# A quantised feed-forward at the end of a four-layer network: its tokens taken by blocks and eighths, its rounding on ScalarE

## The reference, cut to what matters

```python
def _affine_quantize(x):
    amin, amax = (jnp.min(x), jnp.max(x))
    scale = jnp.maximum((amax - amin) / 255.0, 1e-08)
    zp = jnp.clip(jnp.round(-amin / scale) + QMIN, QMIN, QMAX)
    q = jnp.clip(jnp.round(x / scale) + zp, QMIN, QMAX)
    return (q, scale, zp)

def _qlinear(x, W, b):
    xq, sx, zx = _affine_quantize(x)
    wq, sw = _sym_quantize(W)
    acc = jnp.einsum('bsh,oh->bso', xq - zx, wq)
    return acc * (sx * sw) + b
h = _qlinear(x, W1, b1)          # 256 -> 1024 features
h = jax.nn.gelu(h, approximate=False)
out = _qlinear(h, W2, b2)        # 1024 -> 256 features
...
x = x + _L3_ffn_ref(_L3_cond_ref(x, ...), W1, b1, W2, b2)
```

## Time and profile before

| | us |
|---|---|
| three runs | 2984.24, 2985.74, 2986.35 |
| the profiled execution | 2986.55 |
| its span, first to last instruction | 2985.2 |
| from the last extreme of y3 (2895.9) to the end of the span | 89.3 |
| of these, VectorE busy | 72.2 |

### The profile page before, as it was taken

One profiled execution on the slowest core, in us unless ns is written; L12 is line 12 of the kernel. 1 busy time (PEld: TensorE's weight loads), 2 busy tenths in 40 slices (PEclk: granted clock), 3 DMA queues, 4 the chain that ended last, 5 costly groups with the idle time before them and its releaser, 6 DMA issues.

```text
span 2985.2 us, 150990 instructions
## 1 busy us (share of the span) xinstructions
PE 2734.0 (92%) x59732; PEld 2284.0 (77%) x59732; DVE 2077.2 (70%) x12188; ACT 1613.8 (54%) x8443; POOL 338.9 (11%) x457
## 2 busy tenths in 40 slices
PE   7689999999999999999999999998679999979984
PEld 4478999989989899998999989878556666744331
DVE  6688888877777777777777777665456666665238
ACT  3445555566666666666666666543335555511115
POOL 0000101101001010010100101001024444410000
PEclk7555555555555555555555555555589999979997
DMA  3142323212123221231212312101568665251000
GB/s 132 39 118 84 98 73 93 88 38 82 59 75 97 61 83 58 76 92 59 85 55 76 95 57 89 32 14 45 211 222 259 196 193 170 74 175 53 1 0 28
DMA packets 170143, 270.95 MB, mean 91 GB/s; under 512 B 23353, under 2 KB 125644, under 8 KB 167140
## 3 DMA queue, kind: packets, MB, share of 16 engines
q1 hardware_dynamic: 125524, 202.29, 21.6%
q0 software_dynamic: 15312, 33.67, 3.3%
q10 hardware_dynamic: 28608, 25.35, 3.1%
HBM read 170.77 MB, written 98.70 MB: 90 GB/s over the span
## 4 chain that ended last, share of the span: by engine, by line
PE 84%; DVE 8%; ACT 4%; issue 2%; DMA 1%; SPq 0%; POOL 0%; POOLq 0%; ACTq 0%; DVEq 0%
PE work L678 9%; PE bank_h L688 7%; PE bank_r L688 7%; PE bank_z L688 7%; PE bank_g L688 7%; PE bank_h L697 5%; PE work L688 5%; PE bank_r L697 4%; PE bank_z L697 3%; PE bank_g L697 3%; PE work L914 3%; PE bank_z L914 3%; PE bank_h L939 2%; PE work L939 2%; PE work L1025 2%
## 5 line engine op out<-in xcount | busy, mean ns | idle before, releaser
L688 PEld LDWEIGHTS work<-h_run,hi_r 128*128 128x128 f16 x4092 | 258.3, 119 | 164.8 <-DVE h_run L1783 150.0
L688 PE MATMUL work<-h_run,hi_r 128*128 128x2 f16 x4092 | 286.8, 174 | 65.3 <-DVE h_run L1783 60.9
L1783 DVE TENSOR_TENSOR_SCAN h_run<-z_run,hh_run 128x12 f16<-128x12 f32 x1024 | 186.8, 182 | 229.3 <-ACT hh_run L1224 210.5
L1224 ACT ACTIVATE hh_run<-bank_h 128x4 f32<-128x4 f32 x1024 | 179.2, 175 | 275.7 <-PE bank_h L697 275.0
L1205 ACT ACTIVATE r_guess<-work 128x4 f32<-128x4 f32 x1023 | 177.0, 173 | 236.0 <-PE work L688 218.7
L1768 DVE TENSOR_TENSOR_SCAN rh_run<-r_run,h_run 128x12 f16<-128x12 f32 x1023 | 187.1, 183 | 151.5 <-ACT r_run L1214 107.9
L688 PE MATMUL bank_g<-h_hi,hi_g 128*128 128x2 f16 x4092 | 253.4, 166 | 38.7 <-ACT h_hi L1194 38.1
L697 PE MATMUL bank_h<-rh_run,hi_h 128*128 128x2 f16 x4092 | 263.8, 169 | 1.8 <-DVE rh_run L1768 1.2
L1219 ACT ACTIVATE z_run<-bank_z 128x4 f32<-128x4 f32 x1024 | 180.3, 176 | 149.1 <-PE bank_z L697 4.2
L688 PE MATMUL bank_h<-h_run,hi_h 128*128 128x2 f16 x4092 | 253.7, 166 | 3.3 <-DVE h_run L1765 3.3
L697 PE MATMUL bank_g<-h_lo,hi_g 128*128 128x2 f16 x4092 | 253.2, 166 | 1.4 <-DVE h_lo L1746 0.5
(11 more groups left out here) (481 smaller groups left out, 8076.8 us busy)
## 6 DMA issues: line engine op xcount, KB each, us to landing
stage<-in_gate_up SPq DMA_DIRECT2D x128, 384.0 KB
stage<-in_down SPq DMA_DIRECT2D x128, 192.0 KB, 3.0
gu_split<-parts SPq DMA_DIRECT2D x64, 384.0 KB, 2.8
gu_ring<-gu_split SPq DMA_DIRECT2D x64, 384.0 KB
xt<-x_rows ACTq DMA_DIRECT2D x191, 128.5 KB, 2.2
x_rows<-zero_rows SPq DMA_DIRECT2D x64, 257.0 KB, 3.3
yk<-y_rows SPq DMA_DIRECT2D x16, 1024.0 KB, 4.8
dn_split<-parts SPq DMA_DIRECT2D x64, 192.0 KB, 2.7
```

The costliest lines, as they stand in the source:

```text
L688: ins = pe.matmul(o[:, m, step, :], w[:, k, m * P:(m + 1) * P], hi(k), start=False, stop=False, skip_group_check=True)
L1224: act.activation(two(t.hh_run[:, :, 1]), gate_in(t.h, c2, s2), ACT.Tanh, scale=scale_of["h"]).then_inc(s.hh_act, 1)
L1783: dve.tensor_tensor_scan(t.h2_run[:, 0:3 * KH * B], threes(t.z_run), threes(t.hh_run), 0.0, ALU.mult, ALU.add).then_inc(s.h2hi, 1)
```

## The change

- Step 2: ScalarE rounds `y3` block by block (2 x 512 elements a partition) as soon as the inverse is there (a semaphore `inv` on L2017); VectorE clips each block in two passes, and the first of them already writes bfloat16 into `xq`, the second works on `xq` in place. Blocks 2 and 3 are rounded and clipped in the midst of step 3: after the first piece, or pair of pieces, of the block before.
- Step 3: the block is outside and the feature piece inside. VectorE takes an extreme over two feature pieces (2 x 512 elements) in one instruction: 32 reductions.
- Steps 4 and 5: ScalarE rounds `h3` in eighths of the tokens (8 x 256 elements), as soon as the inverse is there; VectorE clips an eighth in two passes, the second in bfloat16. TensorE fills for each eighth the two halves of one bank with 16 matmuls of 256 columns; four banks are used in turn. VectorE multiplies the bank by `f2` and adds `xf` in one instruction for both halves, two eighths behind the clipping. ScalarE no longer evicts; b2 is added to `xf` by ScalarE ahead of step 2 (two instructions of 2048 elements a partition), behind the last Gelu of the layer's experts (L1289).
- The stores go by eighths, 8 of 256 KB as before.

```diff
@@ sync
+    for u in range(8):
+        sp.wait_ge(s.xo, u + 1)
+        sp.dma_start(halves(out)[:, :, eighth(u)], t.xf[:, :, eighth(u)]).then_inc(s.stores, 16)
@@ tensor
     for v in range(NI * NBLK):
-        m, j = divmod(v, NBLK)
+        j, m = divmod(v, NI)
+        if m == 0:
+            pe.wait_ge(s.xq, j + 1)
...
+    for u in range(8):
+        pe.wait_ge(s.hq, u + 1)
+        if u >= 4:
+            pe.wait_ge(s.xo, u - 3)
+        for m in range(KH):
+            for k in range(NI):
+                ins = pe.matmul(work[u % 4][:, m * EIGHTH:(m + 1) * EIGHTH], t.wq3["W2"][:, k, m * P:(m + 1) * P],
+                                t.hq[:, k, eighth(u)], start=(k == 0), stop=(k == NI - 1))
         ins.then_inc(s.o3_mm, 1)
@@ scalar
+    for m in range(KH):
+        act.activation(t.xf[:, m], t.xf[:, m], ACT.Identity, bias=t.b2c[:, m:m + 1])
+    def rounded_input(j):
+        y = t.y3[:, :, blk_cols(j)]
+        act.activation(y, y, ACT.Identity, bias=t.round_col, scale=t.affine["x"]["inv"]).then_inc(s.rounded, 1)
+    act.wait_ge(s.inv, 1)
+    rounded_input(0)
+    rounded_input(1)
     act.wait_ge(s.f1, 1)
     for v in range(NI * NBLK):
-        m, j = divmod(v, NBLK)
+        j, m = divmod(v, NI)
+        if m == 0 and 1 <= j < NBLK - 1:
+            rounded_input(j + 1)
...
-    act.wait_ge(s.f2, 1)
-    for j in range(NBLK):
-        h3 = t.h3[:, :, blk_cols(j)]
-        act.activation(h3, h3, ACT.Identity, bias=t.round_col, scale=t.affine["h"]["inv"]).then_inc(s.hround, 1)
-    for v in range(NBLK * KH):
...
-        act.activation(t.o3[v % 2], t.work[v % 2], ACT.Identity, bias=t.b2c[:, m:m + 1], scale=t.f2).then_inc(s.o3, 1)
+    act.wait_ge(s.inv, 2)
+    for u in range(8):
+        h3 = t.h3[:, :, eighth(u)]
+        act.activation(h3, h3, ACT.Identity, bias=t.round_col, scale=t.affine["h"]["inv"]).then_inc(s.rounded, 1)
@@ vector
+    def to_range(src, dst, tag, quantised):
+        a = t.affine[tag]
+        v.on(dve.tensor_scalar(dst, src, ROUND, a["lo"], ALU.subtract, ALU.max))
+        dve.wait_ge(v.sem, v.n)
+        dve.tensor_scalar(dst, dst, a["hi"], None, ALU.min).then_inc(quantised, 1)
...
+    quantised_input(0)
+    dve.tensor_tensor(t.f1, t.affine["x"]["scale"], t.w3_scale[:, 0:1], ALU.mult).then_inc(s.f1, 1)
+    quantised_input(1)
+    for i in range(NI // 2 * NBLK):
+        j, pair = divmod(i, NI // 2)
+        h3 = t.h3[:, 2 * pair:2 * pair + 2, blk_cols(j)]
+        dve.wait_ge(s.h3, 2 * i + 2)
+        dve.tensor_reduce(t.part[:, 0, i:i + 1], h3, AXXY, ALU.max)
+        v.on(dve.tensor_reduce(t.part[:, 1, i:i + 1], h3, AXXY, ALU.min, negate=True))
+        if pair == 0 and 1 <= j < NBLK - 1:
+            quantised_input(j + 1)
...
+    for u in range(8 + 2):
+        if u < 8:
+            dve.wait_ge(s.rounded, NBLK + u + 1)
+            to_range(t.h3[:, :, eighth(u)], t.hq[:, :, eighth(u)], "h", s.hq)
+        if u >= 2:
+            xc = t.xf[:, :, eighth(u - 2)]
+            dve.wait_ge(s.o3_mm, u - 1)
+            dve.scalar_tensor_tensor(xc, t.work[(u - 2) % 4].rearrange("p (m n) -> p m n", m=KH), t.f2, xc, ALU.mult,
+                                     ALU.add).then_inc(s.xo, 1)
```

More of the change, by code:

```diff
@@ L14 @@
 ACT = mybir.ActivationFunctionType
-AXX = mybir.AxisListType.X
+AXX, AXXY = mybir.AxisListType.X, mybir.AxisListType.XY
 RED = bass.bass_isa.ReduceOp
@@ L44 @@
 E3, H3, S3 = 8, 128, 512
+EIGHTH = N // 8
 NS3 = S3 // P
@@ L66 @@
 blk_cols = lambda j: slice(j * BLK, (j + 1) * BLK)
+eighth = lambda u: slice(u * EIGHTH, (u + 1) * EIGHTH)
 class Steps:
@@ L118 @@
     tb_mm tb router_mm scores comb_sb comb_mm combT sh_mm sg s_in
-    he_mm he_act he o2_mm y3 ext ar xq f1 h3_mm h3 f2 hround hq o3_mm o3 xo stores
+    he_mm he_act he o2_mm y3 ext ar inv rounded xq f1 h3_mm h3 hq o3_mm xo stores
     dve
@@ L429, in place_tiles @@
         t.h3 = sb("h3", [P, NI, N])
-        t.part = sb("part", [P, 2, NI * NBLK])
+        t.part = sb("part", [P, 2, NI // 2 * NBLK])
         t.round_col = sb("round_col", [P, 1])
         t.hq = sb("hq", [P, NI, N], BF16)
-        t.o3 = [sb(f"o3_{i}", [P, BLK]) for i in range(2)]
     dram = lambda name, shape, dt: nc.dram_tensor(name, shape, dt, kind="Internal").ap()
@@ L578, in sync_program @@
         sp.dma_start(t.yk[c % 3].rearrange("p k d -> p (k d)"), results_of[c]).then_inc(yk_sem(s, c), 16)
-    for v in range(NBLK * KH):
[L581 to L584, removed]
+    for u in range(8):
+        sp.wait_ge(s.xo, u + 1)
+        sp.dma_start(halves(out)[:, :, eighth(u)], t.xf[:, :, eighth(u)]).then_inc(s.stores, 16)
+    sp.wait_ge(s.stores, 16 * 8)
 def tensor_program(pe, A, t, s):
@@ L1035, in tensor_layer3 @@
                 ins.then_inc(s.o2_mm, 1)
-    pe.wait_ge(s.xq, 1)
     pe.wait_ge(s.wq3, 1)
     for v in range(NI * NBLK):
-        m, j = divmod(v, NBLK)
+        j, m = divmod(v, NI)
+        if m == 0:
+            pe.wait_ge(s.xq, j + 1)
         if v >= 6:
@@ L2016, in affine @@
         dve.wait_ge(v.sem, v.n)
-        v.on(dve.reciprocal(a["inv"], a["scale"]))
-        dve.wait_ge(v.sem, v.n)
+        dve.reciprocal(a["inv"], a["scale"]).then_inc(s.inv, 1)
+        dve.wait_ge(s.inv, at)
         v.on(dve.tensor_tensor(a["zp"], a["ar"][:, 1:2], a["inv"], ALU.mult))
@@ L2029, in affine @@
         dve.wait_ge(v.sem, v.n)
-    fl, ax = flat(t.y3), t.affine["x"]
+    def to_range(src, dst, tag, quantised):
[3 more added lines that the diff above has]
+        dve.tensor_scalar(dst, dst, a["hi"], None, ALU.min).then_inc(quantised, 1)
+    dve.memset(t.round_col, ROUND)
     dve.wait_ge(v.sem, last)
@@ L2034, in vector_layer3, with quantised_input @@
     affine("x", 1)
[L2035 to L2045, removed]
+    def quantised_input(j):
+        dve.wait_ge(s.rounded, j + 1)
+        to_range(t.y3[:, :, blk_cols(j)], t.xq[:, :, blk_cols(j)], "x", s.xq)
+    quantised_input(0)
[9 more added lines that the diff above has]
+            quantised_input(j + 1)
     dve.wait_ge(v.sem, v.n)
@@ L2048, in vector_layer3 @@
     affine("h", 2)
[L2049 to L2062, removed]
+    f2 = v.on(dve.tensor_tensor(t.f2, t.affine["h"]["scale"], t.w3_scale[:, 1:2], ALU.mult))
+    dve.wait_ge(v.sem, f2)
+    for u in range(8 + 2):
[7 more added lines that the diff above has]
+                                     ALU.add).then_inc(s.xo, 1)
 def gpsimd_program(pool, A, t, s):
```

## The result

The changed kernel takes 2968.14 us, the median of four runs (2966.84 to 2969.86), beside 2985.68 for the kernel before: a ratio of 0.9944 with a 95% interval of 0.9931 to 0.9956. Forecast were 2968.5 us, in a range of 2966.0 to 2975.0. The profiled execution has a span of 2967.8 us in place of 2985.2.

A forecast was written before the change was run, and what follows sets the result against it. VectorE's queue was taken to bound the last 89 us; 5.70 us up to h3's first rounding plus 11.56 in the last stage make 17.3, so 2986.55 goes to 2969.3, median 2968.5, range 2966.0 to 2975.0.

The forecast's parts named there:

- The bound: Last 89 us: VectorE ends last nearly everywhere, 38.13 of 40.10 us among the extremes, 23.89 of 37.30 in the last stage.
- First hand-over: From y3's inverse to the first extreme: block-wise rounding and clipping start the extremes at 2902.46, 4.84 us earlier.
- The extremes: Reductions with two clippings among them: 32 x 1.13 us plus 2.2, stream 38.4 us against 38.06, VectorE not starved.
- rival C: In the extremes: one over two pieces runs at half rate, 2.20 us each, kernel takes 3003 us; chance 3%.
- Second hand-over: From the last extreme to ScalarE's first rounding of h3: 1.33 us in place of 2.53, a gain of 1.20.
- Last stage: From h3's first rounding to the last add: VectorE's pitch 2.57 us per eighth, 23.44 us, before 35.00, gain 11.56.
- The rest: Behind the last add: the store of 256 KB stays at 2.3 us, allowing 0.6 more for its shorter rows.
- The sum: Whole kernel: 5.70 + 11.56 = 17.3 us gained, profiled execution 2969.3 us, median of the runs 2968.5.
- A: In the clippings: the 16-bit pass is no faster than the float32 one, kernel takes 2973.7 us; chance 14%.
- B: In the last stage: TensorE stays at 1.2 GHz and bounds it, 32.3 us, kernel 2977.4; 11% together with D in full.
- D: In the last stage: weight loads surface from under half-width matmuls, 2978.5 us in full (11% with B), 2971.5 by half (7%).

The follow-up runs named there:

- bounds_f32: Changed kernel with the first clipping pass writing float32 again and the second reading it; 76.76 us from first inverse to end, ratio 0.9965 to the kernel before.
- one_piece: Changed kernel with each extreme over 512 elements again, 64 reductions in place of 32; stream 40.43 us, ratio 0.9952 to the kernel before.
- early_two: Changed kernel with block 2 of y3 rounded and clipped ahead of the first extreme; 70.59 us from first inverse to end, ratio 0.9948 to the kernel before.
- four_more: Changed kernel with four more matmuls of 256 columns ahead of each eighth of the second linear layer; last stage 25.33 us, one execution, no ratio.
- changed_again: The changed kernel itself, unaltered, run once more on the experiments' chips; 3040.61 us, ratio 0.9951 to the kernel before.

## Why the prediction was right, point by point

- **The bound.** VectorE's queue sets both stages. Shown: work of a known price was added to the queue (5.06 us in bounds_f32, 1.95 in one_piece) or moved out of the stream (1.16 in early_two), and the end moved by 5.00, 1.93 and 1.17 us.
- **First hand-over.** 5.33 us from the inverse to the first extreme forecast, 5.52 measured; the two passes over block 0 make 0.12 of the difference (0.75 + 0.49 for 0.70 + 0.42), for the reason given at the last stage.
- **The extremes.** Stream 38.40 forecast, 38.50 measured. 1.047 ns an element and a fixed part held from 512 to 2048 elements and over two and four pieces; rival C had no case. That VectorE would not starve was right too: no idle time in the stream.
- **Second hand-over.** 1.33 forecast, 1.29 measured.
- **Last stage.** 23.44 forecast, 24.23 measured: the one term that was noticeably mis-sized. The passes' price by length had as its short end L1872, whose operands are constants; the clippings read the bound from a column. The trace of before has the pair, which I had passed over (groups by shape, with a column operand):

```profile
L1866 DVE TENSOR_SCALAR W<-W,w_inv 128x512 f32<-128x512 f32 x8 | 3.9, 484 | 0.0
```

  484 beside 420 ns. A line through this row and the 2354 ns for 4096 elements, which also has a column, gives 0.75 and 1.29 us for 1024 and 2048; measured were 0.75 and 1.28. For the pass with 16 bits on both sides the forecast had halved the same line, with the same fixed part. Measured in the changed kernel, a pass costs 0.03 and 0.05 us more than forecast at 2048 elements: 8 x 0.083 = 0.66 us, and TensorE's last eighth at 1.92 in place of 1.81 makes 0.1 more.
- **The rest.** From the last add to the end 2.22 for 2.31: rows of half the length cost nothing in the store.
- **The sum.** From the inverse to the end 70.8 us were forecast (5.33 + 38.40 + 1.33 + 23.44 + 2.31) and 71.76 measured, so the gain was forecast 1.0 too large. The median met the forecast within 0.4 us because some 1.1 us of scatter ahead of the inverse went the other way. The mechanism was right; the last digit was luck.
- **The rivals.** A refuted by 753 ns; B by the clock and four_more; D by the step of 0.109 us. The clock in two stretches of the changed kernel's last stage, columns as above:

```profile
2945.60:2949.50 3.90, 3.81 (x18) 2.70 (x19) 3.83 (x5) 3.90 (x3) 0.00 (x0) 0.50 0.00 0
...
2957.00:2965.00 8.00, 6.01 (x51) 4.46 (x48) 7.23 (x10) 0.35 (x1) 0.00 (x0) 1.00 0.30 100
```

  Cold (1.2 GHz) on the first eighths after the rest of 16.29 us, then in full (2.4 GHz), and the pauses of 0.72 us did not lower it. The Trainium skill's kernel that fell back between bursts (TensorE: Matmul & The Clock Gate, "HAM oscillation") is not this case. The Trainium skill's price for a one-source operation with 16 bits on both sides (VectorE: DVE Perf Modes, "The perf-mode tier table"), 693 ns for 2048 elements, is 60 ns under the 753 of the trace, which reads its bound from a column.

## What to carry to other kernels

Find the engine whose queue has no gap and ask of each edit where in that queue its instructions land: the clippings were free ahead of the first extreme (early_two) and cost their full 1.17 us among the extremes. Where a stage is rounding, clipping, multiplying and adding in series, cut it so that fixed parts and the filling of the chain balance: eighths beat quarters by 3.6 us here. And a price by length is drawn through rows of the same operands: one with a constant and one with a column operand are two lines.

## What the runs showed of the hardware that I had not expected

The kernel before took 2986 us in the first measurement and 3055 to 3058 on the three chips of the experiments, 2.4% more. The chip of the first measurement is not on record, so that it is the chip that differs is likely and not shown. The difference lies in the recurrence: from its first `hh_run` to its last there are 1958.2 us in the changed kernel's first trace and 2030.2 in changed_again, 72.0 of the 72.4 between the spans. Between 200 and 2146 us of both traces none of the 42 groups of equal shape with more than 600 instructions differs by more than 1 ns in its mean; the steps are longer. The same 1500 us of the changed kernel, in its first trace and in changed_again, columns as above:

```profile
500.00:2000.00 1500.00, 1457.26 (x41528) 1371.46 (x41529) 1114.80 (x8053) 965.82 (x5888) 114.08 (x193) 0.50 0.23 69
```

```profile
500.00:2000.00 1500.00, 1415.60 (x40201) 1329.97 (x40199) 1082.32 (x7827) 942.11 (x5735) 105.74 (x181) 0.50 0.22 69
```

3.2% fewer matmuls in the same time, and the waits around `r_run` are longer: VectorE's for ScalarE's `r_run` come to 58.7 us in the one and 130.1 in the other, and ScalarE's `r_run` waits 51.0 us for TensorE's `bank_r` in the second, where the first trace lists no such wait. From the first inverse on the two agree within 0.1 us. Why the recurrence is slower there stays open; a stretch of one trace was the better measure of a change at the end than the whole time.
